# Two attention heads per 128-partition stack, one on each row half, with maxima in banks of two and one, and projections spread over a group's steps

## The reference, cut to what matters

```python
h = _modulate(_ln(x), sh_msa, sc_msa)
qkv = (h @ w_qkv + b_qkv).reshape(B, N, 3, nh, hd).transpose(2, 0, 3, 1, 4)
q, k, v = (qkv[0], qkv[1], qkv[2])
attn = jax.nn.softmax(jnp.einsum('bhqd,bhkd->bhqk', q, k) * hd ** (-0.5), axis=-1)
o = jnp.einsum('bhqk,bhkd->bhqd', attn, v).transpose(0, 2, 1, 3).reshape(B, N, C)
o = o @ w_proj + b_proj
x = x + g_msa[:, None, :] * o
...
hmid = jax.nn.gelu(jnp.einsum('tc,ech->eth', xf, w1) + b1[:, None, :], approximate=True)
eo = jnp.einsum('eth,ehc->etc', hmid, w2) + b2[:, None, :]
```

## Time and profile before

| | |
|---|---|
| median of 3 runs | 991.68 us (991.67 to 992.36) |
| the profiled execution | 992.99 us, of which the trace's span is 991.2 us |
| PE, LDWEIGHTS, DVE, ACT, POOL busy over the span | 900.9, 639.9, 566.0, 516.8, 313.3 us |
| attention: first to last exponential | from 109.7 to 565 us |
| its groups 1 to 5 (of 0 to 7), each | 58.8 us |

### The profile page before, as it was taken

The page is one execution under the profiler, slowest core; times in us unless marked ns, Lnnn a source line. Parts: engine busy times, 40 slices in busy tenths (PEclk is TensorE's granted clock), DMA queues, the critical chain, the costliest instruction groups (busy, mean ns, idle before and its releaser), DMA issues. The chain is left out here.

```text
span 991.2 us, 15201 instructions
## 1 busy us (share of the span) xinstructions
PE 900.9 (91%) x5111; PEld 639.9 (65%) x5111; DVE 566.0 (57%) x978; ACT 516.8 (52%) x1003; POOL 313.3 (32%) x314
## 2 busy tenths in 40 slices
PE   4878799999999999999999896438999999999995
PEld 3775444454545545555444375328999999999995
DVE  3767658767676776767774068463455444444342
ACT  1531266777776777777778735435443333333331
POOL 3522111012120111111042149626555444444342
PEclk9898799999999999999999969558999999999998
DMA  8051600624216060330631157405332222222221
GB/s 209 10 114 23 129 3 17 131 84 102 64 27 137 17 128 19 74 84 8 153 98 44 35 162 256 149 25 141 84 60 56 44 43 43 36 41 40 43 36 19
DMA packets 59296, 73.99 MB, mean 75 GB/s; under 512 B 24856, under 2 KB 51334, under 8 KB 58200
## 3 DMA queue, kind: packets, MB, share of 16 engines
q1 hardware_dynamic: 50216, 60.32, 24.5%
q0 software_dynamic: 8400, 12.12, 7.3%
q10 hardware_dynamic: 608, 0.59, 0.2%
HBM read 33.87 MB, written 15.73 MB: 50 GB/s over the span
## 5 line engine op out<-in xcount | busy, mean ns | idle before, releaser
L1014 DVE TENSOR_REDUCE negmax<-m_ps 128x1 f32<-128x1024 f32 x256 | 309.2, 1221 | 129.5 <-PE m_ps L1079 128.8
L1001 ACT ACTIVATE probs<-s_ps 128x512 f32<-128x512 f32 x486 | 282.0, 597 | 102.6 <-PE s_ps L1110 79.8
L1110 PE MATMUL s_ps<-stack 96*128 96x512 f32 x486 | 212.4, 444 | 5.4 <-ACT probs L1001 3.6
L1110 PEld LDWEIGHTS s_ps<-stack 96*128 96x128 f32 x486 | 90.7, 189 | 163.0 <-ACT probs L1001 130.3
L1079 PE MATMUL m_ps<-stack 96*128 96x512 f32 x512 | 167.7, 412 | 13.1 <-DVE negmax L1014 7.4
L449 POOL TENSOR_TENSOR parts<-proj_f,parts 128x512 fp32r<-128x512 f32 x32 | 41.0, 1282 | 322.0 <-ACT proj_f L443 322.0
L1124 PE MATMUL o_ps<-probs,v_aug 128*19 128x512 f32 x1024 | 136.1, 604 | 0.5 <-ACT probs L1001 0.5
L1969 PE MATMUL gate_bank<-weights,ht_hi 128*128 x630 | 127.1, 296 | 0.4 <-DVE ht_lo L1865 0.4
L1079 PEld LDWEIGHTS m_ps<-stack 96*128 96x128 f32 x512 | 97.9, 195 | 35.2 <-DVE negmax L1014 16.7
L1945 PE MATMUL h_ps<-weights,xt_hi 128*128 x525 | 115.7, 351 | 4.1 <-DVE xt_hi L1858 4.1
L1691 ACT CAST ht_hi<-ht_ps 128x384 fp32r<-128x384 f32 x105 | 43.5, 488 | 117.4 <-PE ht_ps L1956 117.4
(11 more groups left out here) (213 smaller groups left out, 1111.7 us busy)
## 6 DMA issues: line engine op xcount, KB each, us to landing
stack<-parts SPq DMA_DIRECT2D x96, 256.0 KB, 5.0
w_raw<-in_L_cond_w SPq DMA_DIRECT2D x9, 432.0 KB, 3.6
w_raw<-in_L_cond_w SPq DMA_DIRECT2D x9, 384.0 KB, 3.4
xn_scratch<-h SPq DMA_DIRECT2D x16, 192.0 KB, 3.7
x_in<-in_x SPq DMA_DIRECT2D x4, 576.0 KB, 9.6
o_scratch<-o_norm SPq DMA_DIRECT2D x16, 144.0 KB, 2.4
o_in<-o_scratch SPq DMA_DIRECT2D x16, 144.0 KB, 2.6
xr<-in_x SPq DMA_DIRECT2D x16, 144.0 KB, 3.1
```

Source lines behind the costliest of these rows:

```text
L1001: nc.scalar.activation(probs[:, st % 2, h], score_bank(g, st, h), ACT.Exp, scale=SCALE)\
L1014: nc.vector.tensor_reduce(negmax[:, half, g % 2, m % 16:m % 16 + 1], m_ps[m % 2][:], AX.X, ALU.max, negate=True).then_inc(max_free, 1)
L1110: nc.tensor.matmul(score_bank(g, st, h), stack[s][:, h, 1, kt // QT, (kt % QT) * P:(kt % QT + 1) * P], stack[s][:, h, 0, half], start=True ...
```

## The change

- **Stacks.** Two heads stand in one 128-partition stack: the even head in rows 0 to 63, the odd one in rows 64 to 127. A head takes 3 x 18 rows of channels, then the two rows of maxima, then rows of ones: `maxima` multiplies 54 rows, `scores` 56. The 12 transfers of a group are 18 rows of 8 KB (or 18 x 2 of 4 KB) in place of 32, and the rows of ones are set by six memsets of 32 x 2048 on POOL: four in `setup`, ahead of the roots of the variances, and two at the start of `attention`. There are three stacks in place of two.
- **Scores.** A slot is two banks, a pair of heads (j = 0, 1), and ACT takes one exponential of 1024 columns for it.
- **Maxima.** A group has 64 blocks of 512 keys. They come in items of two blocks (`m_two`) and of one (`m_one`) by turns; DVE reduces each, and a small reduction (`rowmax`) joins the two key halves. The turns `rows` and `outputs` take a place in the same order, in the same banks.
- **Projections.** No bank of their own: a unit takes a slot of `s_ps`. Units are at steps 2, 5, 9 and 12 (`PROJ_AT`); ACT reads a unit once and POOL makes both parts (a cast and a subtraction).
- **SP's order.** Stack g + 2 is loaded in group g, between the maxima of (g, second half) and those of (g + 1, first half).

```diff
-        self.stacks = [sb(stack, "stack0", [3 * HP, GH, 2, 2, HALF], F32R)]
+        self.stacks = [sb(stack, f"stack{i}", [P, 2, 2, 2, HALF], F32R) for i in range(2)]
...
     def load_stack(self, sp, g):
-        sp.wait_ge(self.parts_ok, 4 * (g + 1))
-
-        n = HP
+        sp.wait_ge(self.parts_ok, self.parts_count(g, 3))
+        sp.wait_ge(self.ones_ok, 2 * min(g + 1, self.STACKS))
         kinds = (slice(self.Q_HI, self.K_HI + 1), slice(self.Q_HI, self.K_LO + 1, 2), slice(self.Q_LO, self.K_HI + 1, 2))
         for h in range(GH):
             for q, kind in enumerate(kinds):
-                sp.dma_start(f32(self.stacks[g % 2][q * HP:q * HP + n, h]).rearrange("p a b n -> p a (b n)"),
-                             f32(self.parts[h * HP:h * HP + n, kind]).rearrange("p a b n -> p a (b n)"))\
+                row = (h % 2) * self.BLOCK + q * HD
+                sp.dma_start(f32(self.stacks[g % self.STACKS][row:row + HD, h // 2]).rearrange("p a b n -> p a (b n)"),
+                             f32(self.parts[h * HP:h * HP + HD, kind]).rearrange("p a b n -> p a (b n)"))\
                   .then_inc(self.stack_ld[h], 16)
...
+            pool.wait_ge(bias_zero, 4)
+            for i in range(2):
+                heads.ones_rows(pool, i)
...
+AHEAD = 48
+RATE = 4
+PROJ_AT = (2, 5, 9, 12)
...
+        self.maxima(self.lead, BLOCKS)
+        self.turn(self.lead, "rows", 0)
+        self.maxima(self.lead, AHEAD)
+        due = []
+        for t, items in enumerate(self.steps):
+            g, st = t // STEPS, t % STEPS
+            begun = self.block // BLOCKS
+            self.maxima(items, AHEAD + RATE * t + 2)
+            for turn in due:
+                self.turn(items, "rows", turn)
+            if st == KT + 2:
+                self.turn(items, "out", 2 * g)
+            if st == 2 and g >= 1:
+                self.turn(items, "out", 2 * g - 1)
+            self.maxima(items, AHEAD + RATE * (t + 1))
+            due = range(begun, self.block // BLOCKS)
...
-        s_ps = [pb(ctx, f"s_ps{i}", [P, HALF]) for i in range(2)]
-        m_ps = [pb(ctx, f"m_ps{i}", [P, N]) for i in range(2)]
+        s_ps = [pb(ctx, f"s_ps{i}", [P, 2, HALF]) for i in range(2)]
+        m_two = pb(ctx, "m_two", [P, 2, HALF])
+        m_one = pb(ctx, "m_one", [P, HALF])
         o_ps = pb(ctx, "o_ps", [P, HALF])
-        misc = pb(ctx, "misc", [P, HALF])
...
             load_w(2)
             load_rows_of_max(0, 0)
+            load_stack(1)
             for g in range(GG):
-                if g + 1 < GG:
-                    load_stack(g + 1)
-                if g == 0:
-                    load_rows_of_max(0, 1)
-                else:
-                    load_rows_of_max(g, 1)
+                load_w(g + 3)
+                if g >= 1:
                     store(g - 1, 1)
+                load_rows_of_max(g, 1)
+                if g + 2 < GG:
+                    load_stack(g + 2)
...
+                store(g, 0)
                 if g + 1 < GG:
                     load_rows_of_max(g + 1, 0)
-                store(g, 0)
                 if g == GG - 2:
                     for i in (2, 3):
                         late.load_piece(sp, 0, i)
-                load_w(g + 3)
...
+            def parts(g, u):
+                half, a = u // 2, u % 2
+                hi, lo = ((heads.Q_HI, heads.Q_LO), (heads.K_HI, heads.K_LO))[a]
+                pool.wait_ge(slot_free, 2 + proj_item(g, u) + 1)
+                if u == 0:
+                    for h in range(GH):
+                        pool.wait_ge(stack_ld[h], 48 * g)
+                nc.gpsimd.tensor_copy(heads.parts[:, hi, half], heads.proj_f[:, u % 2]).then_inc(parts_ok, 1)
+                pool.wait_ge(parts_ok, heads.parts_count(g, u) - 1)
+                nc.gpsimd.tensor_tensor(heads.parts[:, lo, half], heads.proj_f[:, u % 2],
+                                        f32(heads.parts[:, hi, half]), ALU.subtract).then_inc(parts_ok, 1)
...
+            def project(g, u):
+                k = proj_item(g, u)
+                act.wait_ge(slot_mm, k + 1)
+                act.wait_ge(parts_ok, heads.parts_count(g, u) - 4)
+                nc.scalar.activation(heads.proj_f[:, u % 2], s_ps[k % 2][:, 0], ACT.Identity,
+                                     bias=wqk[3][:, g, u % 2:u % 2 + 1]).then_inc(slot_free, 1)
+
+            def exponentials(g, st, j):
+                k = score_item(g, st, j)
+                act.wait_ge(slot_mm, k + 1)
+                if j == 0:
+                    act.wait_ge(pv_free, 16 * g + st + 1)
+                nc.scalar.activation(probs[:, st % 2, 2 * j:2 * j + 2], s_ps[k % 2][:], ACT.Exp, scale=SCALE)\
+                  .then_inc(slot_free, 1)
...
+                src = m_two[:, 0:count] if n % 2 == 0 else m_one[:].unsqueeze(1)
+                nc.vector.tensor_reduce(negmax[:, half, first:first + count], src, AX.X, ALU.max, negate=True)\
+                  .then_inc(max_free, 1)
+                if first + count == BLOCKS:
+                    dve.wait_ge(max_free, 2 + n + 1)
+                    nc.vector.tensor_reduce(rowmax[:, half].rearrange("p (h b) -> p b h", h=2),
+                                            negmax[:, half].rearrange("p (b k h) -> p b h k", k=2, h=2), AX.X, ALU.min)\
+                      .then_inc(rowmax_ok, 1)
...
+                                     (first + i) // (4 * QT))
+                    r = slice(hh * heads.BLOCK, hh * heads.BLOCK + heads.MAX_ROW)
+                    bank = m_two[:, i] if n % 2 == 0 else m_one[:]
+                    mm = nc.tensor.matmul(bank, stack[s][r, j, 0, half, qt * P:(qt + 1) * P], stack[s][r, j, 1, kh],
...
+            def scores(g, st, j):
+                half, kt, s, k = st // KT, st % KT, g % heads.STACKS, score_item(g, st, j)
                 if kt == 0:
-                    pe.wait_ge(rows_ld[half], 32 * (g + 1))
...
+                    pe.wait_ge(rows_ld[half], 64 * (g + 1))
+                pe.wait_ge(slot_free, k + 1)
+                for hh in range(2):
+                    r = slice(hh * heads.BLOCK, hh * heads.BLOCK + heads.MAX_ROW + 2)
+                    mm = nc.tensor.matmul(s_ps[k % 2][:, hh], stack[s][r, j, 1, kt // QT, (kt % QT) * P:(kt % QT + 1) * P],
...
+                    items = plan.steps[STEPS * g + st]
+                    for j in range(PAIRS):
+                        scores(g, st, j)
+                    for it in items[:1]:
+                        item(*it)
                     if st >= 1:
                         values(g, st - 1)
                     elif g >= 1:
                         values(g - 1, STEPS - 1)
-                    scores(g, st, (2,))
-                    for tile in tiles[1:2]:
-                        maximum(*tile)
-                    scores(g, st, (3,))
-                    for tile in tiles[2:]:
-                        maximum(*tile)
-                    for turn in row_turns:
-                        rows(*turn)
-                    for turn in out_turns:
-                        outputs(*turn)
-                    for unit in units:
-                        project(*unit)
+                    for it in items[1:2]:
+                        item(*it)
+                    unit = PROJ_AT.index(st) if st in PROJ_AT and g + 2 < GG else None
+                    if unit is not None:
+                        project(g + 2, unit, slice(0, 4))
+                    for it in items[2:]:
+                        item(*it)
+                    if unit is not None:
+                        project(g + 2, unit, slice(4, len(PRODUCTS)))
```

More of the change, by code:

```diff
@@ new lines, with score_item, proj_item, __init__ @@
+BLOCKS = 2 * GH * QT
+AHEAD = 48
+RATE = 4
+PROJ_AT = (2, 5, 9, 12)
+UNITS = len(PROJ_AT)
+def score_item(g, st, j):
+    before = sum(2 * STEPS + UNITS * (i + 2 < GG) for i in range(g))
+    return UNITS + before + 2 * st + j + sum(st > at for at in PROJ_AT if g + 2 < GG)
+def proj_item(g, u):
+    return u if g == 1 else score_item(g - 2, PROJ_AT[u], 1) + 1
+class MaxPlan:
+    def __init__(self):
+        self.lead, self.steps, self.last = [], [[] for _ in range(STEPS * GG)], []
+        self.rows_at, self.out_at, self.count, self.block = {}, {}, 0, 0
+        self.maxima(self.lead, BLOCKS)
[14 more added lines that the diff above has]
+            due = range(begun, self.block // BLOCKS)
+        self.turn(self.last, "out", 2 * GG - 1)
+    def maxima(self, items, upto):
+        while self.block < min(upto, 2 * GG * BLOCKS):
+            room = BLOCKS - self.block % BLOCKS
+            n = 2 if self.count % 2 == 0 and room >= 2 else 1
+            if self.block + n > upto:
+                break
+            items.append((self.count, "max", self.block // BLOCKS, self.block % BLOCKS, n))
+            self.block, self.count = self.block + n, self.count + 1
+    def turn(self, items, kind, turn):
+        (self.rows_at if kind == "rows" else self.out_at)[turn] = self.count
+        items.append((self.count, kind, turn, 0, 0))
+        self.count += 1
```

(35 more changed lines are left out.)

312 lines of the change are left out of this document (114 added, 198 removed).

## The result

The changed kernel takes 1089.86 us (median of 4 runs, 1089.42 to 1090.71) against 992.02 of the kernel before beside it: ratio 1.0984, 95% interval 1.0965 to 1.1003, 98 us slower. The forecast was 1036, which is 44 us slower than the kernel before and 54 short of what came. The direction was right, the size of the change less than half of what came; the time lies inside the stated range (986 to 1095), near its upper end.

The account below looks back on a forecast made before the run. PE was taken to set the pace of groups 1 to 6. First exponential 112.7, groups 393, stalls 70, late transfers 22.6, clock 11 and the remainder 426.2 made a 1035.5 span, forecast 1036 us, range 986 to 1095.

Parts of the forecast that it names:

- their 22.6: Late transfers for later stages, standing in the group-boundary gaps of SP's queue, add 22.6 us in all.
- The rival that the maxima would not be kept waiting: Small transfers in SP's queue go out faster, stall 4.9 us: 989, or 980 with shorter steps; chance 0.12.
- the second rival: PE's row halves do not overlap: a step takes 3.3 us, a group 61.3, total 1098; chance 0.12.
- the third and the fourth: Attention step rivals: slower bank ring, 3.1 us a step, 1078, chance 0.10; DVE's own pace, 2.31, 1004, chance 0.06.
- a plain step: An attention step without unit or turn takes 2.65 us, against 3.3 before.
- One of the forecast's own signs of being wrong: A setup that ends later than 70 us would show the forecast wrong.
- The stall: PE, ACT and DVE wait on SP's queue 11.65 us at each of six group boundaries, 70; bounds 9.7 and 15.4.
- four units ... together 6.5: A group's four projection units add 6.5 us: seven matmuls 1.6 and slot wait 0.6 each, partly covered by DVE waits.
- the start: Setup's dozen takes 8.1 us, attention begins at 69.9, and the first exponential comes at 112.7.
- the 11 put down for the clock: Low clock after the idle gap costs 1.8 us at each of six group boundaries, 11 together.
- what follows attention: The stages behind attention stay untouched at 426.2 us.
- 59 ahead of SP's queue: Attention's groups gain 62.3 us, the start gives back 3.0: 59 gained before counting SP's queue.

Follow-up runs that it names:

- run 1: Changed kernel with store and the next group's first-half maxima ahead of the stack transfers in SP's queue: 955.6 us.
- run 10: Changed kernel with units at steps 1, 4, 7, 10 instead of 2, 5, 9, 12: 1059.4 us.
- run 2: Changed kernel with the transfers for later stages moved behind the maxima of the next group's first half: 1070.2 us.
- run 8: Kernel 1 with an item's two maxima blocks as two key halves of one head, so both matmuls lie on one row half: 970.7 us.
- Runs 3, 5 and 11: Each on the changed kernel: 16 rows a stack transfer, 1094.8 us; half the bytes a row, 1053.4 us; heads in turns, 1065.2 us (one run).
- Run 7: Kernel 1 with one product instead of seven in every unit made in attention: 938.1 us.
- kernel 1: The kernel of run 1: changed kernel with store and next first-half maxima ahead of the stack transfers, 955.6 us.
- run 3: Changed kernel with 16 instead of 18 rows in each stack transfer: 1094.8 us.

## Why the prediction was right or wrong

**Right, shown by a run:** that SP's queue, with the dozen ahead of the next half's maxima, turns a gain into a loss (run 1: 134 us by the order alone); that it is counted from the unit of step 12 (run 10); that late transfers in that gap are paid for (run 2). That their 22.6 came so near to the measured 23.7 is luck: I priced them as in the kernel before and let all of it count. They take 33.2 behind the dozen, and 9.5 of that costs nothing. The rival that the maxima would not be kept waiting is struck by six gaps.

**Right, shown by the trace:** the two row halves overlap (run 8 gives it a price), which strikes the second rival; a plain step is 2.67 on average (2.65 forecast), which strikes the third and the fourth; group 7 is 37.2 (37). One of the forecast's own signs of being wrong came: the setup's dozen is issued at 73.5, not by 70.

**Wrong, the step that failed:** the sizes of two terms of the sum, both cheap in the forecast, make up 49 of the 52.

- *The stall, "11.65 us at each of six group boundaries: 70".* It is 16.7 each, 100.0, above my upper bound of 15.4. Of the 5.0 more, 3.5 are the dozen: I chose 10.0 between the price by bytes and the price by count, and it is 13.5, the upper end. I reasoned that fewer bytes must be cheaper. Runs 3, 5 and 11 point to what neighbouring rows carry, and that is 8 KB a row before and after: fewer rows changed nothing, half the bytes in a row or another order of the heads took 3.6 to 3.8 off. The other 1.5 are mostly the store and the writes behind a full queue: at the first boundary `store` took 1.31 and the writes 2.2, and it was 5.3 from the dozen's end to the first read, where I had put 3.4.
- *"four units ... together 6.5".* They cost 9.1 in each of groups 1 to 5 (run 1: 54.6 with units, 45.5 without). The whole group is 54.6 against 51.5; of these 3.1, 2.6 are the units and 0.5 the rest, which group 6 shows too (45.5 against 45). Over all eight groups it is 18.7 (run 1's 416.6, less 4.9 that are group 3's alone, against 393). I had let DVE's waits cover part of seven matmuls: 1.35, 2.3, 1.5 and 1.3 for the four units in the order of the forecast (steps 5, 9, 2, 12), where some 2.1, 2.6, 2.4 and 2.0 came. Run 7 shows that 1.06 of 1.4 us of products counts; most of the rest is the slot's hand-over: 0.85 on PE, and behind it 1.72 in which DVE has nothing to reduce.

The rest: the start is 3.5 late, as its dozen takes 13.6 as well (60 to 73.5) instead of 8.1; restarting behind the gaps costs 3.4 more than the 11 put down for the clock (426.1 without gaps, against 416.6 in run 1, less that run's 4.9 in group 3, is 14.4), which fits the 36.3 us at the low level; and what follows attention is 4.7 shorter. 30.0 + 1.1 + 18.7 + 3.5 + 3.4 - 4.7 = 52.0.

I had put down the 4.7 as unchanged. Nearly all of it lies between the last exponential and the last transpose for the output projection, in the kernel before and in the changed one:

```profile
564.97:604.30 39.33, 34.30 (x173) 27.03 (x174) 25.31 (x76) 16.90 (x47) 18.76 (x25) 0.78 0.61 180
666.09:701.20 35.11, 30.12 (x172) 23.65 (x173) 24.70 (x76) 16.60 (x47) 18.70 (x25) 0.90 0.67 203
```

The work is the same, and the granted clock is 0.90 instead of 0.78. That the clock is the cause is argued from that, not shown.

The gain that the change was seen to bring, 59 ahead of SP's queue, is there: kernel 1 is 36 faster than the kernel before, with 18.7 of the 59 lost in the groups, 2.7 at the start and 4.9 in group 3, and 4.6 won behind attention (by the spans it is 37.6).

## What to carry to other kernels

When a change makes an engine's work shorter, read the queue that feeds the next stretch in its new order, and add up all that stands ahead of the short transfer which someone waits for; put the transfer with the nearest reader first. Take the price of a smaller transfer from a row with as many bytes in each row, not from its total bytes: here 144 KB took as long as 256 KB. Work that shares a buffer with the scores costs its own time and one hand-over (2.3 us for 1.6 of matmuls).

## What the runs showed of the hardware

- Two prices of a transfer on SP. The first three of a dozen took 0.59 to 0.69 us with 32 or 16 rows and 0.78 to 0.84 with 18; most of the later ones took 1.2 to 1.3, with 16, 18 or 32 rows of 8 KB alike. At 18 rows the engines' share was 0.49, at 16 it was 0.90. The Trainium skill (DMA: Bandwidth & Descriptors, Why a DMA increments its semaphore by 16 and not by 1) says that a transfer uses the largest number of engines up to 16 that divides its slowest dimension. For 18 rows that is 9, a share of 0.56 at most, an estimate by that page, which the 0.49 fits. That fewer engines cost time was my theory, and run 3 refutes it here.
- What 8 KB a row costs: the Trainium skill (SBUF — State Buffer, Door 1: The DMA port swizzle) says that four neighbouring partitions share one port and gives 27.2 GB/s for it. Four rows of 8 KB by that are 1.20 us, an estimate beside the measured 1.24; that half the bytes in a row brought a transfer down to SP's own 0.8 fits the rule. That it is the port, and not something else that neighbouring rows share, no run isolates.
- A transfer that is issued is not yet moved: with the heads in turns SP was through the dozen 3.8 us sooner, and at the end of group 1 it waited 5.3 us from the small write's issue to the read, against 2.7. With no dozen just ahead (run 1, 216.01 to 217.05) it is 1.0.
- The clock: behind gaps of 16.6 to 26.4 us the granted clock stood at 0.50 for 3.3 to 9.7 us of nearly unbroken work, and in run 3 for up to 15.7. In run 7 group 0, which has no gap, had 0.75 on average: the clock was 0.50 from 73.6 to 138.4 us, though PE was busy 9.90 of the 10 us from 120 to 130.
